# A loop over two blocks of a Mamba and feed-forward layer, written out in full

## The reference, cut to what matters

```
xz = x @ W_in.T ; x_ssm, z = split(xz)
x_ssm = silu(causal_conv4(x_ssm) + conv_b)
proj = x_ssm @ W_x.T ; B, C = 16 columns each ; dt = softplus(proj[-1] * W_dt + b_dt)
h[t] = exp(dt[t] * A) * h[t-1] + (x[t] * dt[t]) * B[t] ; y[t] = sum_n h[t] * C[t]
y = (y + x_ssm * D) * silu(z) ; x1 = layernorm(x + y @ W_out.T)
u = silu(x1 @ w1.T * s1) * (x1 @ w2.T * s2)
u = gelu(u @ h1.T * t1) ; u = gelu(u @ h2.T * t2)
out = layernorm(x1 + u @ w3.T * s3)
```

## Time and profile before

| | |
|---|---|
| median of three runs | 1143.42 us |
| profiled execution | 1143.2 us |
| its span, first to last instruction | 1141.4 us |
| granted clock of TensorE, mean | 0.968 |
| matmul records of TensorE | 4928 |
| HBM read | 146.08 MB |

### The profile page before, as it was taken

How to read it: one execution, slowest core, us unless ns; L and a number is a source line. 1 busy time by engine, 2 the same in 40 slices (tenths; PEclk the granted TensorE clock), 3 DMA queues, 4 the chain that set the end, 5 groups by cost and what they waited for, 6 DMA issues and landing times.

```text
span 1141.4 us, 16943 instructions
## 1 busy us (share of the span) xinstructions
PE 1034.3 (91%) x4928; PEld 646.8 (57%) x4928; DVE 1030.4 (90%) x1484; ACT 903.7 (79%) x1257; POOL 887.5 (78%) x561
## 2 busy tenths in 40 slices
PE   4655999999999999999989999999999999998997
PEld 2434566565656556565655656565565656555543
DVE  4999999998999989999899989999899999989511
ACT  7664989888898978989798888889789798978231
POOL 1667878889697978979698887978789797889640
PEclk8677999999999999999999999999999999999999
DMA  5661340705216070522507062250705225070000
GB/s 182 265 244 71 134 173 10 315 11 230 96 63 252 14 311 9 219 106 88 229 9 315 9 243 84 82 233 13 313 9 215 109 87 229 12 305 2 18 10 10
DMA packets 44065, 152.13 MB, mean 133 GB/s; under 512 B 4560, under 2 KB 24016, under 8 KB 27728
## 3 DMA queue, kind: packets, MB, share of 16 engines
q1 hardware_dynamic: 43600, 151.02, 33.8%
q10 hardware_dynamic: 384, 0.32, 0.1%
HBM read 146.08 MB, written 5.24 MB: 133 GB/s over the span
## 4 chain that ended last, share of the span: by engine, by line
PE 56%; issue 15%; ACT 11%; POOL 9%; DVE 7%; DMA 1%; POOLq 0%; ACTq 0%; DVEq 0%
PE G L707 26%; PE Y L692 11%; POOL pb L322 5%; ACT dA L337 5%; PE G L714 3%; DVE hb L600 3%; ACT g L380 3%; PE G L729 3%; PE Y L655 2%; PE G L675 2%; PE G L711 2%; DVE U L593 2%; POOL r L288 2%; PE Y L737 1%; PE G L659 1%
## 5 line engine op out<-in xcount | busy, mean ns | idle before, releaser
L322 POOL TENSOR_TENSOR pb<-hb,cbc 128x1024 f32<-128x1024 f32 x256 | 602.0, 2363 | 165.8 <-DVE hb L600 165.8
L600 DVE TENSOR_TENSOR_SCAN hb<-dA,U 128x512 f32<-128x512 f32 x512 | 594.6, 1204 | 0.0
L337 ACT ACTIVATE dA<-dt,negA 128x510 f32<-128x510 f32 x512 | 343.6, 713 | 95.5 <-DVE hb L600 73.1
L593 DVE TENSOR_TENSOR U<-X,bbc 128x512 f32<-128x512 f32 x512 | 327.0, 685 | 28.8 <-issue 19.0
L692 PEld LDWEIGHTS Y<-ident,pb 128*128 128x128 f32 x2048 | 241.8, 145 | 122.8 <-issue 70.9
L692 PE MATMUL Y<-ident,pb 128*128 128x128 f32 x2048 | 271.5, 280 | 39.5 <-POOL pb L322 39.4
L707 PE MATMUL G<-hid,h_sb 128*128 128x512 f32 x512 | 234.1, 601 | 2.3 <-ACT g L399 1.6
L707 PE MATMUL G<-g,h_sb 128*128 128x512 f32 x512 | 229.8, 593 | 0.0
L707 PEld LDWEIGHTS G<-hid,h_sb 128*128 128x128 f32 x512 | 96.6, 194 | 113.4 <-issue 108.3
L707 PEld LDWEIGHTS G<-g,h_sb 128*128 128x128 f32 x512 | 92.6, 190 | 94.5 <-issue 91.5
L288 POOL TENSOR_SCALAR r<-r,mv,rs 128x128 f32<-128x128 f32 x124 | 96.8, 794 | 6.6 <-POOL rs L281 6.6
(11 more groups left out here) (90 smaller groups left out, 952.0 us busy)
## 6 DMA issues: line engine op xcount, KB each, us to landing
cbc<-scr SPq DMA_DIRECT2D x64, 1024.0 KB, 9.4
bbc<-scr SPq DMA_DIRECT2D x63, 1024.0 KB, 9.9
xT_sb<-xT_d SPq DMA_DIRECT2D x16, 256.0 KB, 2.8
xtok_sb<-xtok_d SPq DMA_DIRECT2D x16, 256.0 KB, 2.8
out_d<-r SPq DMA_DIRECT2D x16, 256.0 KB, 2.4
h_sb<-h_d SPq DMA_DIRECT2D x2, 1024.0 KB, 22.6
bbc<-scr SPq DMA_DIRECT2D x2, 512.0 KB, 4.8
scr<-rows SPq DMA_DIRECT2D x62, 16.0 KB, 1.5
```

Source lines behind the costliest of these rows:

```text
L322: nc.gpsimd.tensor_tensor(pb[:, qs:qs + 2, :], hb[:, hs:hs + 2, :], cbc[:, n:n + 2, :], ALU.mult).then_inc(s_p, 1)
L337: nc.scalar.activation(halves(dA[:, u % DA_RING, :])[:, :, 1:SEQ], halves(dt[:, par, c, :])[:, :, 1:SEQ], ACT.Exp, scale=negA[:, c, n:n + ...
L593: nc.vector.tensor_tensor(U[i][:], X[:], bbc[:, n + i, :], ALU.mult).then_inc(s_u, 1)
L600: nc.vector.tensor_tensor_scan(hb[:, 2 * (v % H_PAIRS) + i, :], dA[:, u % DA_RING, :], U[i][:], 0.0, ALU.mult, ALU.add).then_inc(s_h, 1)
```

## The change

The loop of `rounds` is no longer a loop on the engines but one in Python: the twelve blocks j = 2 to 13 are written out, one after another, and j is a number. With it each wait of these blocks is for a constant, and each transfer has a constant address. The banks, buffers, operations and their order are the same.

```
-        def rounds(eng, run):
+        def rounds(run):
             run(0, 0, True, True, True, False, False)
             run(1, 1, True, True, True, True, False)
-            with eng.Fori(0, (NB - 4) // 2) as i:
+            for i in range((NB - 4) // 2):
                 run(i * 2 + 2, 0, True, True, True, True, True)
                 run(i * 2 + 3, 1, True, True, True, True, True)
             run(NB - 2, 0, True, False, True, True, True)
...
-            rounds(sp, run)
+            rounds(run)
```

More of the change, by code:

```diff
@@ L323, in run @@
                                                 ALU.mult).then_inc(s_p, 1)
-            rounds(pool, run)
+            rounds(run)
         @block.scalar
@@ L528, in run @@
                         fill_X(A, 0)
-            rounds(act, run)
+            rounds(run)
         @block.vector
@@ L648, in run @@
                         taps(I, 1)
-            rounds(dve, run)
+            rounds(run)
         @block.tensor
@@ L876, in run @@
                         hidden(BH2[2], h2_sb, 2, g1, s_g1, s_h2, F)
-            rounds(pe, run)
+            rounds(run)
 def kernel(L0_attn_x, L0_attn_W_in, L0_attn_conv_w, L0_attn_conv_b, L0_attn_W_x, L0_attn_A_log, L0_attn_D_param,
```

## The result

The written-out kernel takes 1127.01 us (median of four runs, 1126.13 to 1127.65) against 1144.05 us for the kernel before on the same chips: a ratio of 0.9849, 95% interval 0.9832 to 0.9866. The forecast was 1126.8. The profiled execution took 1127.65 us, with a span of 1125.8.

What follows compares the result with a forecast made beforehand. Without jumps, TensorE plus 8 us on ScalarE bounds a block at 64.60 us, VectorE 0.28 behind. 167.61 + 775.20 + 3.4 + 178.6 + 1.8 = 1126.6, median 1126.8; eight-in-ten range 1122.8 to 1132.0.

Steps and rivals of the forecast that it cites:

- The jumps: Five jumps back to the loop's head, stalling VectorE and ScalarE, all go: +17.24 us over twelve blocks.
- Registers at nothing: Loop waits counted from registers become constants: taken as 0, at most 0.2 us; out_proj to dt_proj 22.54 us either way.
- What is late next: After the stall goes, nothing new is late: the joint from j = 3 to 4 takes 64.60 us.
- the ring through TensorE and ScalarE: Chain from in_proj through dt_proj, then ScalarE's rows, softplus, decay and gT to next in_proj: 56.54 + 8.06 = 64.60 us.
- VectorE's 64.32: Length of the block after a jump, where VectorE never waits: the most it needs, 0.28 us behind the 64.60.
- The clock: TensorE's clock falls after the 2.0 us pause before in_proj: two falls guessed, 3.4 us, bounds none to five (8.6 us).
- the 1.1 us of before: Cost of a clock fall in the kernel before, read as 65.70 - 64.60, against 1.7 us without slack.
- The sum: Profiled execution: head 167.61 + blocks 775.20 + clock falls 3.4 + tail 178.6 + 1.8 around = 1126.6 us; median 1126.8.
- Exposed loads of straight code: Rival: loading written-out code stalls at block joints, 3.45 us each; at all twelve 1167.6 us; chance 3%.
- the stall only stood in for another wait: Rival: the jump's stall covers a wait for X or a broadcast that comes anyway; time stays 1143.4 us; chance 2%.

Runs made afterwards that it cites:

- the exchange on TensorE: Hidden 1's feed-forward matmuls moved ahead of in_proj at TensorE's step 10: 1120.57 us in the written-out kernel, 1138.23 us in the kernel before with its loop.
- the turned loop: Against the written-out kernel, only VectorE loops, its two-block trip starting at step 8, so jumps fall where broadcasts rest: 1129.02 us.
- the lighter broadcasts: From block 1 on each B and C broadcast moves 256 KB instead of 1 MB: kernel before with loop 1139.03 us, written-out kernel 1127.62 us.

## Why the prediction was right, step by step

*The jumps.* Shown: kernels that differ in the number of jumps order as five, two, one and none (1144, 1135.6, 1130.7, 1127.0), and the loss comes back with VectorE's loop alone. Which engine's stall counts was open in the prediction: it reckoned with VectorE's time, but named ScalarE as stalled beside it. ScalarE's 20.8 us were worth nothing, because it works up to six scans ahead and makes the stall up (the timeline above).

*Registers at nothing.* Shown: 64.60 us with registers and with constants.

*What is late next.* All written-out blocks at full clock take 64.60 or 64.61 us, and the exchange on TensorE shows that it is the ring through TensorE and ScalarE, read from the earlier trace rows, that sets it. VectorE's 64.32 stood right behind it, as the 64.33 to 64.38 of the exchange show.

*The clock.* I took two falls of 1.7 us, called it a guess, and the profile had two of 1.70 and 1.69. That the number fits is luck within 0 to 5; in other profiled kernels without jumps or with harmless ones it was one to two (ScalarE looping: one; TensorE, POOL and SP looping: two), and none where the exchange has filled the pause. The size was read from the earlier trace rows and held. That a fall costs more in a block without slack was right as well, but the 1.1 us of before was read against the wrong block: all three blocks of 65.7 follow a jump, and their like at full clock takes 64.32, so there a fall cost 1.4 us. The sum is not touched by it.

*The sum.* 168.73 + 778.64 + 178.43 + 1.85 = 1127.65 for the profiled execution, against 167.61 + 778.6 + 178.6 + 1.8 = 1126.6. What is off by 1.1 us is the head, blocks 0 and 1, which the change doesn't touch; it lies between 166.6 and 169.0 us in the profiles of these kernels. That the median is within 0.2 us of the forecast is partly luck: the forecast put the median 0.2 us above the profiled execution, and it came 0.6 below.

*The rivals.* Exposed loads of straight code: none on any engine of the written-out kernel, though the instruction queues moved 76 packets. But the thought behind this rival, that code is loaded through the broadcasts and held up by them, fits the turned loop, 1.2 us at rest and 3.8 us among the broadcasts, and in part the lighter broadcasts. It hurt only after a jump; why straight code among the same broadcasts is spared, no run here shows. That the stall only stood in for another wait is refuted by the same rows as the forecast is borne out.

## What to carry to other kernels

Look at which engine's stall the block can't absorb, and write out the loop on that engine: here VectorE alone gave the whole 17 us, and the four others could keep loops and registers. Where a loop must stay, try turning it so that the jump falls where the transfers rest; with VectorE's loop alone kept, that brought 1144 to 1129. And read the ring behind a small pause of the busiest engine: 2 us of waiting a block hid behind two engines at over 90%, and filling it with the next work in line gave 6.4 us more, about half of it by falls of the clock that no longer came.

## What the runs showed that I had not expected

TensorE's loop of two blocks, the longest of all, is jumped back over without a gap and without more packets on q8 (15 in five kernels); VectorE's of 309 and ScalarE's of 256 listed instructions stall for 3.8 and 4.2 us among the broadcasts, and the loops of POOL (159) and SP (60) bring no packets. With trips of four and six blocks TensorE stalls too, 2.5 to 2.75 us, and its clock falls with it. So a longer trip has fewer jumps but dearer ones, 4.4 to 4.7 us instead of 3.45. And two engines that stall at the same moment for the same reason are not worth the same: one of the two was free.
